# Order of the last inverse groups and four patch-row buffers in a two-layer convolution and spectral-gating kernel

## The chip, the cores and the metric

The kernel runs on one core of one Trainium2 chip. The metric is the device time of one execution in microseconds (us), the median of several runs. The kernel is one program for the five engines of the core, each with its own in-order queue: TensorE (PE in the profile), VectorE (DVE), ScalarE (ACT), GpSimd (POOL) and SyncE (SP), which issues all DMAs. They wait for each other on semaphores alone.

## The reference, cut to what matters

The input is x of shape (16, 32, 128, 128), float32. Layer 0 is a depthwise 3x3 convolution with weights mixed per image, and a 1x1 convolution. Layer 1 is the one that the change touches:

```python
def _L1_conv_ref(x, w_hidden, w_dw, norm_w, norm_b, w_out, patch_size):
    hidden = jnp.einsum('oc,bchw->bohw', w_hidden, x)          # 32 -> 192 channels
    hidden = conv(hidden, w_dw, 3x3, depthwise, 'SAME')
    q, k, v = jnp.split(hidden, 3, axis=1)                     # 64 channels each
    q_fft = jnp.fft.rfft2(to_patch(q))                         # patches of 8 x 8 pixels
    k_fft = jnp.fft.rfft2(to_patch(k))
    out = jnp.fft.irfft2(q_fft * k_fft, s=(p, p))
    mu, var = out.mean(axis=1), out.var(axis=1)                # over channels, per pixel
    out_norm = (out - mu) / jnp.sqrt(var + 1e-05) * norm_w + norm_b
    gated = v * out_norm
    return jnp.einsum('oc,bchw->bohw', w_out, gated)

x = x + _L0_conv_ref(_gn(x), ...)
x = x + _L1_conv_ref(_gn(x), ...)
```

## The kernel before, in words

The first phase (about the first 560 us) does layer 0 for all 16 images and stores the normalised result, split in a high and a low float16 part, padded, to DRAM. The second phase does layer 1 in 32 units, u = 0 to 31, each of half an image: 8 patch rows of 16 patches. Transforms are done as matmuls, on windows of 10 x 10 pixels (a patch and its border), so that the depthwise convolution is folded into the matrices `G_q` and `G_k`.

A unit has two halves on every engine, written out by hand in the functions `front` and `spectral`:

- `front(u, half, tail)` makes the hidden channels of unit u and at the same time finishes unit u - 1, the tail. VectorE's `window` (line 1099) copies one patch row of 16 overlapping windows from `xs` into a buffer `win`; there are two, and the copy of row r first waits until the hidden groups of row r - 2 are done. TensorE's `hidden_group` (line 558), four groups for each patch row, 32 in all, multiplies it; ScalarE (line 811) moves the result into `hwin`. For the tail, VectorE takes pixel statistics of `Y` (line 1109), hands the variance to POOL for the root (lines 1115 and 441), centres (1122) and scales (1129) in eight pieces p = 0 to 7; TensorE's `turn` (line 590) transposes a piece, ScalarE (820) copies it to `gated`, VectorE's `gate` (1134) multiplies it by v, and TensorE's `project` (599) applies `w_out`; VectorE's `residual` (1141) adds it to the image. v itself comes from `v_chunk` (line 577), 18 matmuls of 512 columns for each of eight chunks, into three banks in turn. Between the taps of a chunk stand the hidden groups.
- `spectral(u, half, tail)` transforms q (line 637, eight octets) and k (line 654, sixteen quads), VectorE multiplies them (line 1199, sixteen products, two for each of four buffers `prod`), TensorE transforms back (line 670, `inverse_octet`, eight groups), and ScalarE copies the result to `Y` (line 865). Groups 0 to 5 stand in pairs between the quads. Behind the last quad TensorE does `v_chunk` 0 of this unit, with the wait for the last product and for `Y` ahead of its last tap, then groups 6 and 7. VectorE copies patch rows 0 and 1 of the next unit behind products 8 and 11.

`front` of TensorE then goes on with two hidden groups, `v_chunk` 1 with four more between its taps, `turn` of piece 0, `v_chunk` 2 with five, `turn` of piece 1, and so on; a `project` stands ahead of `turn` 2, 4 and 6, and `turn` 7 stands behind the first q octet of `spectral`. `v_chunk` 1 and 2 wait for ScalarE's last two copies to `Y`, since these share their banks; later chunks wait for the gate of the chunk two before; a `project` waits for both gates that it uses. In the order before, VectorE's front copies patch row 2 behind the scale of piece 0, row 3 behind the scale of piece 1, and rows 4 to 7 at the ends of steps p = 1 to 4, each behind that step's gate, centre, scale and, where there is one, residual.

The first unit has no tail: its copies stand beside the last statistics of the first phase. The last `front` has no hidden groups and only finishes unit 31.

Of the kernel before, what the change touches and what calls it, by code (L numbers as in the profile page):

```python
# [63 lines left out]
def build(nc, t, out):  # L64
# [22 lines left out]
    with ctx:  # L87
# [177 lines left out]
        hwin = take(128 * 128)  # L265
        Y = take(64 * 64)
        q_sb = [take(512) for _ in range(2)]
        prod = [take(1024) for _ in range(4)]
        gated = [take(512) for _ in range(2)]
        res = take(2048)  # L270
        xs_1, xs_0 = [take(HALF * WP, f16) for _ in range(2)]
# [1 line left out]
        assert stage1_end <= top[0] - (HALF * WP + 1) // 2  # L273
        G_q = take(64 * 64)
        G_k = take(64 * 128)
        win = [take(1632, f16) for _ in range(2)]

        block = ctx.enter_context(nc.Block())
# [126 lines left out]
        @block.gpsimd  # L406
        def _(pool):

            pool.memset(powers, -0.5).then_inc(s_pool_consts, 1)
            pool.memset(ones_row, 1.0).then_inc(s_pool_consts, 1)  # L410
            for s in range(3):
                pool.memset(xq[s][0:32, 0:W], 0.0).then_inc(s_x_edges, 1)
                pool.wait_ge(s_x_edges, 2 * s + 1)
                pool.memset(xq[s][96:128, (BAND - 1) * W:BAND * W], 0.0).then_inc(s_x_edges, 1)
                pool.wait_ge(s_x_edges, 2 * s + 2)
            pool.wait_ge(s_prep_v, 1)
            pool.memset(xh.bitcast(f32), 0.0).then_inc(s_pads_zero, 1)
            pool.memset(xl.bitcast(f32), 0.0).then_inc(s_pads_zero, 1)
            for s in range(2):
                pool.memset(win[s][:, 16 * WIN:1632].bitcast(f32), 0.0).then_inc(s_win_room, 1)  # L420
            pool.wait_ge(s_pool_consts, 2)
            pool.wait_ge(s_pads_zero, 2)
            pool.wait_ge(s_win_room, 2)

            for b in range(-1, NB + 1):
                pool.wait_ge(s_ve, b + 2)
                pool.tensor_tensor(tiny["rstds"], tiny["ve"], powers[:, 0:2], ALU.pow).then_inc(s_rstd, 1)
                pool.wait_ge(s_rstd, b + 2)
                if b + 1 < NB:
                    pool.wait_ge(s_centred, 4 * (b + 1) + 1)  # L430
                    pool.memset(xq[(b + 1) % 3][0:32, 0:W], 0.0).then_inc(s_halo_zero, 1)
                    pool.wait_ge(s_halo_zero, 2 * (b + 1) + 1)
                    pool.wait_ge(s_centred, 4 * (b + 1) + 4)
                    pool.memset(xq[(b + 1) % 3][96:128, (BAND - 1) * W:BAND * W], 0.0).then_inc(s_halo_zero, 1)
                    pool.wait_ge(s_halo_zero, 2 * (b + 2))
# [13 lines left out]
        def _(pe):  # L449
# [94 lines left out]
            def hidden_group(u, g, ring):  # L544
# [6 lines left out]
                    pe.wait_ge(s_x2_ready, NCH * NB)  # L551
                if positive(32 * u + g + 1 - ring):
                    pe.wait_ge(s_h_ready, 32 * u + g + 1 - ring)
                w = win[g // 4 % 2]
                for i in range(4):
                    first = (4 * (g % 4) + i) * WIN
                    for low, high in ((0, 64), (64, WIN)):
# [4 lines left out]
            def v_chunk(u, half, k, jr, groups, between, before_last=None):  # L562

                chunk = 2 * k + jr
                if chunk == 0:
# [3 lines left out]
                if chunk > 2:  # L569
                    pe.wait_ge(s_gated, 8 * u + chunk - 2)  # L570
                for tap in range(9):
                    if tap == 8 and before_last is not None:
                        before_last()
                    dy, dx = tap // 3, tap % 3
                    for s in range(2):
                        row = 8 * (2 * s + jr) + dy
# [52 lines left out]
            def spectral(u, half, tail):  # L629
# [36 lines left out]
                def inverse_octet(m):  # L666
                    for part in range(2):
                        for par in range(2):
                            for lam in range(2):
                                mm = pe.matmul(i_banks[par][64 * lam:64 * lam + 64, 256 * (m % 2):256 * (m % 2) + 256],  # L670
                                               small["inverse"][64 * par:64 * par + 64, 64 * part:64 * part + 64],
                                               at(prod[m % 4][64 * par:64 * par + 64, :], 256 * part + 64 * lam, [512, 2], [128, 2], [1, 64]),
                                               start=part == 0, stop=part == 1)
                    mm.then_inc(s_inverse_mm, 1)

# [4 lines left out]
                for m in range(8):  # L680
# [8 lines left out]
                    k_quad(2 * m + 1)  # L689
                    if m == 0 and tail is not None:  # L690
                        project(tail, 3)
                v_chunk(u, half, 0, 0, 0, None, lambda: inverse_inputs(7))
                inverse_octet(6)
                inverse_octet(7)

            front(0, 0, None)
            spectral(0, 0, None)
# [184 lines left out]
        def _(dve):  # L882
# [209 lines left out]

            def window(u, half, r, b=None):

                if positive(32 * u + 4 * (r - 1)):
                    dve.wait_ge(s_hidden_mm, 32 * u + 4 * (r - 1))
                if r == 0:
                    dve.wait_ge(s_xs_in[half], 64 * (b + 1))
                dve.tensor_copy(win[r % 2][:, 0:16 * WIN].rearrange("p (j y x) -> p j y x", y=10, x=10),  # L1099
                                     at(xs[half], 8 * r * WP, [8, 16], [WP, 10], [1, 10])).then_inc(s_win_ready, 1)  # L1100

            def pixel_stats(u, p):
# [38 lines left out]
                dve.tensor_tensor(piece, banks[6].rearrange("p (l r w) -> p l r w", l=2, r=8), piece, ALU.add).then_inc(s_res_done, 1)  # L1141

            def front(u, half, tail):
                rows = iter(range(2, 8) if u is not None else ())

                def windows(n=1):
                    for r in islice(rows, n):
# [2 lines left out]
                if tail is None:  # L1150
                    second_stats(NB - 1, range(4, NCH))
                    aggregate(NB + 2, NB - 1, None)
                    windows(2)
                    quarter_variance(NB + 2, None)
                    low(NB - 2, 0)
                    low(NB - 2, 1)
# [11 lines left out]
                    if p == 1:  # L1168
                        centre(tail, 0)
                scale(tail, 0)  # L1170
                windows()
                centre(tail, 1)
                scale(tail, 1)
                windows()
                for p in range(8):
                    if p < 5:
                        pixel_stats(tail, p + 3)
                        variance(tail, p + 3)
                    if p < 7 or u is None:
                        gate(tail, p // 2, p % 2)  # L1180
                    if p < 6:
# [1 line left out]
                        scale(tail, p + 2)  # L1183
                    if p in (2, 4, 6):
                        residual(tail, p // 2 - 1)
                    if p > 0:
                        windows()

            def spectral(u, tail, nxt):
                if tail is not None:  # L1190
                    gate(tail, 3, 1)
                for n in range(16):
                    m, second = n // 2, n % 2
                    dve.wait_ge(s_q_copied, 8 * u + m + 1)
                    dve.wait_ge(s_k_mm, 16 * u + n + 1)
                    if positive(8 * u + m - 3):
                        dve.wait_ge(s_inverse_mm, 8 * u + m - 3)
                    parts = lambda a: a.rearrange("p (part x) -> p part x", part=2)
                    dve.tensor_tensor(parts(prod[m % 4][:, 512 * second:512 * second + 512]), parts(k_banks[n % 3]),  # L1199
                                      q_sb[m % 2][:, 256 * second:256 * second + 256].unsqueeze(1).broadcast_to([128, 2, 256]),  # L1200
                                      ALU.mult).then_inc(s_prod_ready, 1)
                    if n == 1 and tail is not None:
                        residual(tail, 3)
                    if nxt is not None and n in (8, 11):
                        window(nxt[0], nxt[1], (n - 8) // 3, nxt[2])

            dve.wait_ge(s_win_room, 2)
            window(0, 0, 0, 0)
            window(0, 0, 1, 0)
# [54 lines left out]
```

## Time and profile before

| | |
|---|---|
| median of three runs | 2808.57 us |
| lowest and highest | 2798.39 and 2824.54 us |
| the profiled execution's own time | 2816.34 us |
| its span, first to last instruction | 2814.5 us |
| TensorE matmuls busy | 2513.6 us, 89% |
| VectorE, ScalarE, GpSimd busy | 59%, 51%, 17% |
| mean granted TensorE clock | 0.965 of full speed |

Shares are of the span. Matmuls are pipelined and their ends are modelled, so the busy share of TensorE is no measure of how near to its peak it is. "Idle before" an instruction is the time in which its engine had nothing running ahead of it; the releaser named is what ended that time.

### The profile page before, as it was taken

The numbers are of one execution on the slowest core, as the hardware profiler recorded it, in microseconds if no ns is written. First come the engines' busy times: TensorE is split into PE (matmuls) and PEld (weight loads), VectorE is DVE, ScalarE is ACT, GpSimd is POOL, SyncE is SP. The second block draws the span as 40 slices with busy tenths as digits, with TensorE's granted clock in tenths as the row PEclk, the third lists the DMA queues.
The fourth block names the chain that finished last, engine by engine and source line by source line (L and its number), as shares of the span: only waits on it lengthen the run. The fifth ranks groups of instructions, "written<-read, shape, count | busy, mean of one in ns | idle before, by whom it ended". The sixth has DMA issues, their size and how long they took to land.

```text
span 2814.5 us, 90655 instructions
## 1 busy us (share of the span) xinstructions
PE 2513.6 (89%) x40199; PEld 1659.2 (59%) x40199; DVE 1650.5 (59%) x4058; ACT 1440.8 (51%) x2381; POOL 471.8 (17%) x322
## 2 busy tenths in 40 slices
PE   7888889789999999999999899998999989999998
PEld 3333333466666666666666666666666666666665
DVE  4656666455555555555555556555555555656555
ACT  3545555645455555555555455555555555555552
POOL 1000000021111212112121112122212122212221
PEclk9988988899999999999999999999999999999999
DMA  6788887622222222222222222222222222222221
GB/s 128 184 214 202 213 227 203 165 66 62 57 63 59 63 63 67 63 59 67 59 67 63 59 63 63 63 65 61 67 63 66 61 62 66 68 60 67 63 52 46
DMA packets 60345, 248.30 MB, mean 88 GB/s; under 512 B 12393, under 2 KB 12658, under 8 KB 53714
## 3 DMA queue, kind: packets, MB, share of 16 engines
q1 hardware_dynamic: 59954, 242.50, 35.3%
q8 instruction: 317, 5.19, 0.8%
q14 instruction: 74, 0.61, 0.1%
HBM read 140.74 MB, written 101.72 MB: 86 GB/s over the span
## 4 chain that ended last, share of the span: by engine, by line
PE 58%; DVE 14%; ACT 5%; issue 3%; SPq 0%; DMA 0%; DVEq 0%
PE bank L654 16%; PE bank L577 11%; PE bank L670 9%; PE bank L637 7%; PE bank L590 6%; PE bank L558 5%; ACT arena L820 4%; PE bank L599 4%; DVE arena L1109 3%; DVE arena L1122 3%; DVE arena L1134 2%; DVE arena L1129 2%; DVE arena L1099 2%; DVE arena L1141 2%; ACT arena L865 1%
## 5 line engine op out<-in xcount | busy, mean ns | idle before, releaser
L441 POOL TENSOR_TENSOR arena<-arena 128x8 f32<-128x8 f32 x256 | 447.6, 1748 | 1814.8 <-DVE arena L1115 1809.8
L577 PE MATMUL bank<-arena 128*64 128x512 f16 x4608 | 713.4, 403 | 5.5 <-ACT arena L865 5.5
L811 ACT ACTIVATE arena<-bank 100x512 f32<-100x512 f32 x1024 | 615.7, 630 | 183.8 <-PE bank L558 166.7
L1199 DVE TENSOR_TENSOR arena<-bank,arena 128x512 f32<-128x512 f32 x512 | 354.1, 692 | 457.4 <-PE bank L654 370.6
L558 PEld LDWEIGHTS bank<-arena 128*36 128x36 f16 (+1 forms) x8192 | 332.0, 106 | 382.5 <-DVE arena L1099 157.8
L654 PE MATMUL bank<-arena 100*64 100x128 f32 x8192 | 513.1, 274 | 15.4 <-issue 8.7
L558 PE MATMUL bank<-arena 128*36 128x128 f16 (+1 forms) x8192 | 406.1, 224 | 122.1 <-DVE arena L1099 115.8
L654 PEld LDWEIGHTS bank<-arena 100*64 100x64 f32 x8192 | 457.5, 136 | 54.4 <-issue 47.3
L512 PE MATMUL bank<-arena 32*32 32x508 f32 (+1 forms) x9216 | 389.7, 660 | 57.7 <-issue 42.9
L820 ACT ACTIVATE arena<-bank,arena 128x256 f32<-128x256 f32 x512 | 261.1, 560 | 191.6 <-PE bank L590 189.6
L865 ACT ACTIVATE arena<-bank 128x512 f32<-128x512 f32 x256 | 139.1, 596 | 406.1 <-PE bank L670 406.1
L1134 DVE TENSOR_TENSOR arena<-arena,bank 128x512 f32<-128x512 f32 x256 | 176.0, 687 | 270.1 <-ACT arena L820 268.7
L857 ACT ACTIVATE arena<-bank 128x512 f32<-128x512 f32 x256 | 149.2, 598 | 338.6 <-PE bank L637 325.2
L1109 DVE BATCH_NORM_STATS2 arena<-arena 128x6 f32<-128x128 f32 x1024 | 221.9, 279 | 139.2 <-ACT arena L865 139.2
L637 PE MATMUL bank<-arena 100*64 100x128 f32 x4096 | 274.3, 275 | 4.7 <-ACT arena L857 3.2
L512 PEld LDWEIGHTS bank<-arena 32*32 32x32 f32 x9216 | 142.7, 108 | 207.2 <-issue 177.2
L577 PEld LDWEIGHTS bank<-arena 128*64 128x64 f16 x4608 | 211.2, 112 | 87.8 <-ACT arena L865 11.0
L670 PE MATMUL bank<-arena 64*64 64x256 f32 x4096 | 254.8, 383 | 1.3 <-issue 1.3
L637 PEld LDWEIGHTS bank<-arena 100*64 100x64 f32 x4096 | 233.2, 137 | 30.6 <-issue 17.9
L590 PE MATMUL bank<-arena 128*128 128x128 f32 x1024 | 181.9, 301 | 66.6 <-DVE arena L1129 59.9
L590 PEld LDWEIGHTS bank<-arena 128*128 128x128 f32 x1024 | 133.8, 195 | 167.2 <-DVE arena L1129 101.2
L670 PEld LDWEIGHTS bank<-arena 64*64 64x64 f32 x4096 | 143.6, 131 | 84.4 <-issue 32.7
(112 smaller groups left out, 1620.6 us busy)
## 6 DMA issues: line engine op xcount, KB each, us to landing
arena<-xn_d SPq DMA_DIRECT2D x128, 536.2 KB, 8.3
xn_d<-arena SPq DMA_DIRECT2D x130, 260.0 KB, 4.5
x_d<-arena SPq DMA_DIRECT2D x64, 512.0 KB, 8.3
arena<-x_d SPq DMA_DIRECT2D x128, 256.0 KB, 4.9
out<-arena SPq DMA_DIRECT2D x128, 256.0 KB, 5.3
arena<-x_in SPq DMA_DIRECT2D x32, 544.0 KB, 10.1
arena<-x_in SPq DMA_DIRECT2D x32, 528.0 KB, 10.0
arena<-spectra_in SPq DMA_DIRECT2D x1, 1152.0 KB
```

What stands on the lines that cost most here:

```text
L441: pool.tensor_tensor(tiny["rstd"][:, slot], tiny["var_eps"][:, slot], powers, ALU.pow).then_inc(s_root, 1)
L512: mm = pe.matmul(at(psum_of(t, r)[32 * c:32 * c + 32, :], low, [W, 4], [1, high - low]), conv_w[b % 2][32 * r:32 * r + 32, 32 * tap:32 * t ...
L558: mm = pe.matmul(banks[g % ring][low:high, 128 * i:128 * i + 128], w[:, first + low:first + high], hidden_w, start=True, stop=True)
L577: mm = pe.matmul(v_banks[chunk % 3][64 * s:64 * s + 64, :], v_w[:, 64 * tap:64 * tap + 64], at(xs[half], row * WP + 32 * k + dx, [32 * WP, ...
L590: tr = pe.transpose(t_bank[:, 128 * i:128 * i + 128], at(Y, 8 * k + 4 * jr + i, [32, 128]), ident)
L637: mm = pe.matmul(banks[m % 2][64 * par:64 * par + 64, 128 * pair:128 * pair + 128], G_q[0:WIN, 64 * ch:64 * ch + 64], hwin[0:WIN, 128 * ch ...
L654: mm = pe.matmul(k_banks[n % 3][64 * par:64 * par + 64, 256 * part + 128 * pair:256 * part + 128 * pair + 128], G_k[0:WIN, 128 * ch + 64 * ...
L670: mm = pe.matmul(i_banks[par][64 * lam:64 * lam + 64, 256 * (m % 2):256 * (m % 2) + 256], small["inverse"][64 * par:64 * par + 64, 64 * pa ...
L811: act.activation(h_rows[0:WIN, :, first:first + 4], banks[g % ring][0:WIN, :].rearrange("p (i c) -> p c i", i=4), ACT.Copy).then_inc(s_h_r ...
L820: ins = act.activation(at(gated[jr], 256 * lam, [32, 8], [8, 4], [1, 8]), at(banks[4], 64 * lam, [8, 8], [128, 4], [1, 8]), ACT.Identity, ...
L1109: ins = dve.bn_stats(T["pixel_stats"][:, first:first + 6], at(Y, 2048 * s + 4 * p + j, [32, 64], [1, 2]))
L1199: dve.tensor_tensor(parts(prod[m % 4][:, 512 * second:512 * second + 512]), parts(k_banks[n % 3]), q_sb[m % 2][:, 256 * second:256 * secon ...
```

## The change

TensorE: behind the last k quad the last two inverse groups come at once, each behind its own wait, and `v_chunk` 0 follows them. VectorE: four `win` buffers instead of two, so the copy of row r waits for the hidden groups of row r - 4. Rows 0 to 3 of the next unit are copied behind products 8, 10, 11 and 13, row 4 behind the scale of piece 1, and rows 5 to 7 in steps p = 1 to 3, now ahead of that step's gate. Products go round three buffers instead of four, and wait for one inverse group more. For the first unit rows 0 to 3 are copied ahead of `front`.

```diff
-        prod = [take(1024) for _ in range(4)]
+        prod = [take(1024) for _ in range(3)]
...
-        win = [take(1632, f16) for _ in range(2)]
+        win = [take(1632, f16) for _ in range(4)]
...
@@ hidden_group
-                w = win[g // 4 % 2]
+                w = win[g // 4 % 4]
@@ v_chunk
-                    if tap == 8 and before_last is not None:
-                        before_last()
@@ inverse_octet
-                                               at(prod[m % 4][64 * par:64 * par + 64, :], ...),
+                                               at(prod[m % 3][64 * par:64 * par + 64, :], ...),
@@ spectral, TensorE
-                v_chunk(u, half, 0, 0, 0, None, lambda: inverse_inputs(7))
+                pe.wait_ge(s_prod_ready, 16 * u + 14)
+                pe.wait_ge(s_y_ready, 8 * u + 6)
                 inverse_octet(6)
+                pe.wait_ge(s_prod_ready, 16 * u + 16)
                 inverse_octet(7)
+                v_chunk(u, half, 0, 0, 0, None)
@@ window
-                if positive(32 * u + 4 * (r - 1)):
-                    dve.wait_ge(s_hidden_mm, 32 * u + 4 * (r - 1))
+                if positive(32 * u + 4 * (r - 3)):
+                    dve.wait_ge(s_hidden_mm, 32 * u + 4 * (r - 3))
@@ front, VectorE
-                rows = iter(range(2, 8) if u is not None else ())
+                rows = iter(range(4, 8) if u is not None else ())
...
                     aggregate(NB + 2, NB - 1, None)
-                    windows(2)
                     quarter_variance(NB + 2, None)
...
                 scale(tail, 0)
-                windows()
                 centre(tail, 1)
                 scale(tail, 1)
                 windows()
                 for p in range(8):
                     if p < 5:
                         pixel_stats(tail, p + 3)
                         variance(tail, p + 3)
+                    if p > 0:
+                        windows()
                     if p < 7 or u is None:
                         gate(tail, p // 2, p % 2)
...
                         residual(tail, p // 2 - 1)
-                    if p > 0:
-                        windows()
@@ spectral, VectorE
-                    if positive(8 * u + m - 3):
-                        dve.wait_ge(s_inverse_mm, 8 * u + m - 3)
+                    if positive(8 * u + m - 2):
+                        dve.wait_ge(s_inverse_mm, 8 * u + m - 2)
...
-                    if nxt is not None and n in (8, 11):
-                        window(nxt[0], nxt[1], (n - 8) // 3, nxt[2])
+                    if nxt is not None and n in (8, 10, 11, 13):
+                        window(nxt[0], nxt[1], (8, 10, 11, 13).index(n), nxt[2])
```

## Rows read from the trace of the kernel before

**Rows 1.** The page: granted clock in 40 slices; shares of the chain that ended last.
```profile
PEclk9988988899999999999999999999999999999999
...
PE 58%; DVE 14%; ACT 5%; issue 3%; SPq 0%; DMA 0%; DVEq 0%
```

**Rows 2.** Waits of TensorE, 700 to 2600 us: total, times, longest.
```profile
PE bank L558 <- DVE arena L1099: 97.2, 81, 1.6
PE bank L590 <- DVE arena L1129: 49.8, 27, 1.9
...
PE bank L577 <- ACT arena L865: 4.2, 27, 0.2
```

**Rows 3.** Timeline of TensorE in one unit: start, length, what, [idle before, releaser].
```profile
1437.28 2.23 PE L577 MATMUL bank<-arena 128*64 128x512 f16 x18
1439.44 1.98 PE L670 MATMUL bank<-arena 64*64 64x256 f32 x32
1441.34 0.64 PE L558 MATMUL bank<-arena 128*64 128x128 f16 x16
1442.13 0.88 PE L577 MATMUL bank<-arena 128*64 128x512 f16 x6 [0.15 <-ACT arena L865]
...
1447.12 0.71 PE L590 MATMUL bank<-arena 128*128 128x128 f32 x4 [1.85 <-DVE arena L1129]
...
1454.90 1.02 PE L599 MATMUL bank<-arena 128*64 128x512 f32 x4
...
1459.25 0.39 PE L577 MATMUL bank<-arena 128*64 128x512 f16 x2
1460.89 0.41 PE L558 MATMUL bank<-arena 128*64 128x128 f16 x8 [1.25 <-DVE arena L1099]
...
1465.66 0.41 PE L558 MATMUL bank<-arena 128*64 128x128 f16 x8 [0.88 <-DVE arena L1099]
...
1471.90 0.41 PE L558 MATMUL bank<-arena 128*64 128x128 f16 x8 [1.47 <-DVE arena L1099]
...
1478.51 0.68 PE L590 MATMUL bank<-arena 128*128 128x128 f32 x4 [0.18 <-ACT arena L820]
```

**Rows 4.** Timeline of VectorE in the same unit.
```profile
1435.81 0.69 DVE L1199 TENSOR_TENSOR arena<-bank,arena 128x512 f32<-128x512 f32 x1 [2.24 <-PE bank L654]
...
1437.55 0.69 DVE L1199 TENSOR_TENSOR arena<-bank,arena 128x512 f32<-128x512 f32 x1 [0.18 <-PE bank L654]
1442.60 0.88 DVE L1109 BATCH_NORM_STATS2 arena<-arena 128x6 f32<-128x128 f32 x4 [4.36 <-ACT arena L865]
...
1446.38 0.69 DVE L1129 TENSOR_TENSOR arena<-arena 128x512 f32<-128x512 f32 x1
1446.98 0.57 DVE L1099 COPY arena<-arena 128x1600 f16<-128x1600 f16 x1
...
1452.91 0.87 DVE L1109 BATCH_NORM_STATS2 arena<-arena 128x6 f32<-128x128 f32 x4
...
1460.27 0.57 DVE L1099 COPY arena<-arena 128x1600 f16<-128x1600 f16 x1
```

**Rows 5.** Timeline of ScalarE in the same unit.
```profile
1434.74 1.09 ACT L865 ACTIVATE arena<-bank 128x512 f32<-128x512 f32 x2 [2.20 <-PE bank L670]
```

**Rows 6.** Timeline of GpSimd in the same unit.
```profile
1445.55 4.44 POOL L441 TENSOR_TENSOR arena<-arena 128x8 f32<-128x8 f32 x2
...
1451.07 1.64 POOL L441 TENSOR_TENSOR arena<-arena 128x8 f32<-128x8 f32 x1 [1.09 <-DVE arena L1115]
```

**Rows 7.** Stretches: all 31 units, one undisturbed unit, two at the lower clock.
```profile
core 0: us, PE busy (x) PEld busy (x) DVE busy (x) ACT busy (x) POOL busy (x), PEclk, DMA share, GB/s
595.35:2773.48 2178.13, 1989.09 (x29760) 1419.54 (x29756) 1283.14 (x3098) 1114.76 (x1984) 434.25 (x248) 0.99 0.26 62
1441.48:1510.51 69.03, 63.26 (x966) 45.30 (x964) 41.44 (x100) 35.80 (x65) 14.17 (x8) 1.00 0.27 64
670.89:674.30 3.41, 3.41 (x36) 2.13 (x34) 1.86 (x6) 2.12 (x4) 1.65 (x1) 0.50 0.02 5
2500.44:2503.85 3.41, 3.41 (x29) 1.92 (x30) 1.68 (x4) 2.21 (x4) 1.90 (x1) 0.50 0.00 0
```

More of the change, by code:

```diff
@@ L418, in _ @@
             pool.memset(xl.bitcast(f32), 0.0).then_inc(s_pads_zero, 1)
-            for s in range(2):
+            for s in range(4):
                 pool.memset(win[s][:, 16 * WIN:1632].bitcast(f32), 0.0).then_inc(s_win_room, 1)
@@ L422, in _ @@
             pool.wait_ge(s_pads_zero, 2)
-            pool.wait_ge(s_win_room, 2)
+            pool.wait_ge(s_win_room, 4)
             for b in range(-1, NB + 1):
@@ L560, in hidden_group, with v_chunk @@
                 mm.then_inc(s_hidden_mm, 1)
-            def v_chunk(u, half, k, jr, groups, between, before_last=None):
+            def v_chunk(u, half, k, jr, groups, between):
                 chunk = 2 * k + jr
@@ L671, in inverse_octet @@
                                                small["inverse"][64 * par:64 * par + 64, 64 * part:64 * part + 64],
-                                               at(prod[m % 4][64 * par:64 * par + 64, :], 256 * part + 64 * lam, [512, 2], [128, 2], [1, 64]),
+                                               at(prod[m % 3][64 * par:64 * par + 64, :], 256 * part + 64 * lam, [512, 2], [128, 2], [1, 64]),
                                                start=part == 0, stop=part == 1)
@@ L1093, in window @@
             def window(u, half, r, b=None):
-                if positive(32 * u + 4 * (r - 1)):
-                    dve.wait_ge(s_hidden_mm, 32 * u + 4 * (r - 1))
+                if positive(32 * u + 4 * (r - 3)):
+                    dve.wait_ge(s_hidden_mm, 32 * u + 4 * (r - 3))
                 if r == 0:
                     dve.wait_ge(s_xs_in[half], 64 * (b + 1))
-                dve.tensor_copy(win[r % 2][:, 0:16 * WIN].rearrange("p (j y x) -> p j y x", y=10, x=10),
+                dve.tensor_copy(win[r % 4][:, 0:16 * WIN].rearrange("p (j y x) -> p j y x", y=10, x=10),
                                      at(xs[half], 8 * r * WP, [8, 16], [WP, 10], [1, 10])).then_inc(s_win_ready, 1)
@@ L1195, in spectral @@
                     dve.wait_ge(s_k_mm, 16 * u + n + 1)
-                    if positive(8 * u + m - 3):
-                        dve.wait_ge(s_inverse_mm, 8 * u + m - 3)
+                    if positive(8 * u + m - 2):
+                        dve.wait_ge(s_inverse_mm, 8 * u + m - 2)
                     parts = lambda a: a.rearrange("p (part x) -> p part x", part=2)
-                    dve.tensor_tensor(parts(prod[m % 4][:, 512 * second:512 * second + 512]), parts(k_banks[n % 3]),
+                    dve.tensor_tensor(parts(prod[m % 3][:, 512 * second:512 * second + 512]), parts(k_banks[n % 3]),
                                       q_sb[m % 2][:, 256 * second:256 * second + 256].unsqueeze(1).broadcast_to([128, 2, 256]),
@@ L1203, in spectral @@
                         residual(tail, 3)
-                    if nxt is not None and n in (8, 11):
-                        window(nxt[0], nxt[1], (n - 8) // 3, nxt[2])
-            dve.wait_ge(s_win_room, 2)
-            window(0, 0, 0, 0)
-            window(0, 0, 1, 0)
+                    if nxt is not None and n in (8, 10, 11, 13):
+                        window(nxt[0], nxt[1], (8, 10, 11, 13).index(n), nxt[2])
+            dve.wait_ge(s_win_room, 4)
+            for r in range(4):
+                window(0, 0, r, 0)
             front(0, 0, None)
```

## The prediction

> **What bounds the kernel now.** I first read the busy line of the clock and the chain that ended last [rows 1]: the clock is at its upper level outside the first fifth, and over half of the chain is TensorE, with VectorE second. The kernel spends 2178.13 us of its 2814.5 us in 31 equal units of the second phase [rows 7]; the stretch before them (595 us) and after them (41 us) is hardly touched by the diff. A unit without disturbance takes 69.03 us [rows 7]. So the question is what TensorE does in one unit.
>
> The list of waits over 1900 us, 27 units, answers: TensorE waits for the patch-row copies of line 1099 97.2 us (81 times, three in a unit), for `y_norm` of line 1129 49.8 us (27 times) and for ScalarE's Y copies 4.2 us [rows 2]. The timeline of one unit shows the places [rows 3]. Let T0 be the end of the last inverse group, 1441.34. There are 0.15 us of wait before the next `v_chunk`, 1.85 us before the first `turn`, 1.25, 0.88 and 1.47 us before the hidden groups that open patch rows 5, 6 and 7, and 0.18 us before the last `turn`. The spectral half in front of T0 runs without a gap worth naming.
>
> How long is a wait really? Two matmuls start at 1459.25 and the next group at 1460.89 [rows 3]. Two of them cost 0.23 us when others follow directly, so the wait costs 1.41 us and not the recorded 1.25. In the same way 0.88 becomes 1.04, 1.47 becomes 1.63, 1.85 becomes 2.01, and 0.15 becomes 0.34. The Trainium skill says so too (Perfetto Trace Analysis, Identifying the Most-Contended Engine): matmul busy time is a poor measure because matmuls are pipelined. By recorded idle alone the five waits would be worth 5.6 us a unit, by starts 6.4; the trace agrees with the page, and my sum is made from starts.
>
> **Part 1: inverse groups first, then `v_chunk(0)`.** Now `v_chunk(0)` takes 1437.28 to 1439.44, 2.16 us, and the two inverse groups 1.90 us behind it [rows 3]. After T0 a chain starts that no order on TensorE shortens: ScalarE's two copies, VectorE from 1442.60 (statistics, centre, scale), scale at 1446.38 for 0.69 us [rows 4], and `turn` at 1447.12, T0 + 5.78 [rows 3]. TensorE has only 3.4 us of other work for it. With `v_chunk(0)` behind T0 it has 2.16 + 0.45 (two hidden groups) + 2.98 (`v_chunk(1)` with four) = 5.59 us. The chain is still last by about 0.2 us, so `turn` stays at T0 + 5.78, and the whole 2.16 us, now spent in the chain's shadow, is gained.
> What it adds is a wait. Group 6 needs product 14, done at 1435.81 + 0.69 = 1436.50 [rows 4], and Y copies that end at 1435.83 [rows 5], so it starts at 1437.28 and ends near 1438.23. Group 7 needs the last product, 1437.55 + 0.69 = 1438.24 [rows 4]. Everything on TensorE queues behind this wait. A release is followed by TensorE 0.05 us later (1447.07 to 1447.12), and a wait costs some 0.15 us more than it records, as above. So it costs between 0.06 and 0.4 us (a pipeline drain plus a short stall, as the 0.34 of the Y copies); I take 0.15, as the wait is all but met when it is reached. Net gain: 2.0 us.
>
> **Part 2: four patch-row buffers, copies ahead of the gates.** The three waits cost 1.41 + 1.04 + 1.63 = 4.08 us. Does the copy come in time? In the order before, rows 2 and 3 are copied in the busiest stretch of VectorE (1446.98) and row 5 at 1460.27, T0 + 18.93, behind a residual, while TensorE asks for it at 1459.64 [rows 3, 4]. In the new order rows 0 to 3 are done in the spectral half, where VectorE idles 2.24 us before a product [rows 4]. A copy occupies 0.49 us from start to start. The statistics of step 4 start at 1452.91, T0 + 11.57 [rows 4]. Ahead of them two copies and the 0.41 us wait in front of the second fall away and one copy comes: they start at T0 + 10.7, and row 5 is copied at T0 + 11.7. Row 6 follows one step (3.5 us) later, row 7 one more (4.2 us, with a residual and a gate that waits): about T0 + 15.2 and 20.0. TensorE, dense from `turn` on, asks for them at about T0 + 18.3, 21.8 and 26.2. Margins are 6 us, so all three waits go. The waits that the copies themselves carry (4, 8, 12, 16 hidden groups done) are met 3 us or more ahead.
> What is late next? The gates. `project(0)` starts at T0 + 13.56 (1454.90) [rows 3] and needs gate 1, which I get at T0 + 12.1 + 0.7 = 12.8: 0.7 us of margin. The same walk over the orders of the two engines leaves 0.8 and 0.9 us at `project(1)` and `project(2)`, where VectorE itself again waits for ScalarE. The chunk that needs gate 0 has 1.0 us. POOL's second root ends near T0 + 5.9, 0.5 us ahead of its scale. So nothing new shows in TensorE, but nothing is wide.
>
> **Part 3: copies in the spectral half** now behind products 8, 10, 11 and 13. Behind product 13 the copy pushes product 14 from 1436.68 to 1436.91 and product 15 would then be free at 1437.52, before its own quad is done at 1437.55 [rows 4]. Behind product 10 product 11 comes 0.2 us later, while the inverse group that reads it is reached 0.3 us after that. Cost 0, with 0.1 us as the bound. Row 0 waits for the load of the next half image, which was so before at the same product.
>
> **Part 4: three product buffers.** Product m now waits for m - 2 inverse groups. Groups 0 and 1 are done before product pair 4 and groups 2 and 3 before pair 5 is needed; group 4 before pair 7. The wait is met each time by one pair at least: 0. Moved addresses and two more small memsets on POOL at the start: 0; the fourth removed edit, `before_last`, belongs to part 1. In the first unit four copies stand in an idle stretch of VectorE instead of two: 0.
>
> **Sum.** A unit gives 2.0 + 4.08 = 6.1 us; 31 units 189 us; the clock 24 us; T0 of the first unit 2 us earlier; the last front 0 (its chain also ends at T0 + 5.78 + what follows). 215 us from the profiled execution's own 2816.34 us gives 2601 us. That execution lies 8 us above the median of the runs, 2808.57; as the clock's falls differ by chance and mostly go, I take off only a little: 2600 us.
>
> **Rivals.**
> (A) The falls of the clock stay, or a gate margin turns into a short wait. The clock may fall after shorter pauses once they stand alone; against it, no fall follows the three waits of up to 1.47 us. 2601 + 24 = 2625 us; with another 0.3 us in each unit 2634.
> (B) The copies get in each other's way with POOL. The new copies of rows 5 to 7 stand directly behind the statistics that release POOL's root. The rows show that a copy and a root do touch: the two roots that ran beside the copies of patch rows 2 and 3 took 2.22 us each, one with no copy beside it 1.64 [rows 6], but the copy itself was not held (1446.98, 0.57 us, started within a running root) [rows 4]. If copies were held for a whole root, each would come 1.6 us late, the gate behind it too, past the 0.7 us margin: about 1 us for each of three steps, 3 us a unit, 93 us: near 2695 us. The Trainium skill states this rule (SBUF, Who interferes with whom): whichever of a two-port VectorE copy and a GpSimd instruction issues first blocks the other fully. The trace disagrees for the copy here and shows only a partial delay for POOL.
> (C) Part of it only: the copies help, but the wait is moved from `turn` to inverse group 7 or gate 0, so that part 1 gives nothing: 31 x 2.0 = 62 us less and the falls stay: 2687 us. Against it is the count above, 1438.23 against 1438.24.
> (D) Slower: a denser TensorE is not granted the upper clock. Place: the front half, now without pauses. A fall of 3.41 us costs 1.6 us, so it decides between four and five falls in each unit: four (13.6 us of 63 at the lower level) leave 2799 us, five give 2601 + 31 x 5 x 1.6 = 2849 us. Against it: the spectral half is gapless now, and no fall starts in it.
>
> **Chances.** Forecast 0.66, A 0.20, B 0.04, C 0.06, D 0.03, the remaining 0.01 for no change. The range takes the forecast with its bounds (the new wait at 0.4 us adds 8 us; the clock of the first phase and the median 15 us either way) and A: 2582 to 2638 us. Faster by over 1% 0.96, within 1% 0.01, slower 0.03; 1% is about what the spread of the three runs before lets one tell from nothing.
>
> **What would show it.** In the profile after: no TensorE wait for line 1099's copies in the units; the wait at the first `turn` under 0.4 us with `turn` still 5.8 us behind the last inverse group; a new short wait of the inverse groups for the last product; units of 63 us; the clock at its upper level after 600 us. Wrong would be the gate margins, if waits appear at `project`; the clock, if falls go on; and VectorE's walk, if copies are late.

## The result, and the profile after

The changed kernel takes 2595.18 us (median of 4 runs, 2584.55 to 2598.81), the kernel before 2807.22 us (4 runs). The ratio is 0.9231 with a 95% interval of 0.9179 to 0.9284. The profiled execution took 2592.72 us with a span of 2590.9 us, 223.6 us less than that of before.

The page after, busy line of TensorE, granted clock in 40 slices, and shares of the chain that ended last:

```profile
PE 2463.1 (95%) x40199; PEld 1648.5 (64%) x40199; DVE 1638.2 (63%) x4058; ACT 1447.8 (56%) x2381; POOL 476.4 (18%) x324
...
PEclk9989898879999999999999999999999999999999
...
PE 69%; DVE 6%; ACT 2%; issue 1%; SPq 0%; DMA 0%; ACTq 0%
```

Against [rows 1] TensorE's share of the chain has gone from 58% to 69% and VectorE's from 14% to 6%: the chain now stays on TensorE. The waits of TensorE from 700 to 2400 us (total, times, longest):

```profile
PE bank L652 <- issue: 6.5, 5, 1.6
PE bank L588 <- ACT arena L821: 4.8, 27, 0.2
```

Both large entries of [rows 2] are gone. What is left is 0.18 us in each unit at the last `turn` (line 588 now, 590 before) and a few waits for instructions ("issue"). All 31 units, and one undisturbed unit, in the view of stretches:

```profile
core 0: us, PE busy (x) PEld busy (x) DVE busy (x) ACT busy (x) POOL busy (x), PEclk, DMA share, GB/s
591.26:2551.64 1960.38, 1943.09 (x29762) 1408.84 (x29760) 1270.16 (x3096) 1121.86 (x1984) 438.80 (x248) 1.00 0.29 69
1348.82:1411.66 62.84, 62.54 (x962) 45.32 (x961) 41.00 (x100) 36.18 (x65) 14.15 (x8) 1.00 0.30 71
```

A unit takes 62.84 us instead of 69.03, and all 31 take 1960.38 instead of 2178.13 us [rows 7]. One unit in TensorE's timeline (start, length, what):

```profile
1343.96 2.84 PE L652 MATMUL bank<-arena 100*64 100x128 f32 x48
1346.73 2.02 PE L668 MATMUL bank<-arena 64*64 64x256 f32 x32
1348.68 2.25 PE L575 MATMUL bank<-arena 128*64 128x512 f16 x18
1350.77 0.61 PE L558 MATMUL bank<-arena 128*64 128x128 f16 x16
...
1353.95 0.39 PE L558 MATMUL bank<-arena 128*64 128x128 f16 x8
1354.46 0.71 PE L588 MATMUL bank<-arena 128*128 128x128 f32 x4
...
1362.23 1.03 PE L597 MATMUL bank<-arena 128*64 128x512 f32 x4
1363.19 0.71 PE L588 MATMUL bank<-arena 128*128 128x128 f32 x4
...
1366.81 0.39 PE L558 MATMUL bank<-arena 128*64 128x128 f16 x8
...
1370.52 0.39 PE L558 MATMUL bank<-arena 128*64 128x128 f16 x8
...
1375.10 0.39 PE L558 MATMUL bank<-arena 128*64 128x128 f16 x8
```

The last inverse groups come at 1346.73, `v_chunk` 0 and 1's first taps behind them at 1348.68, which is the new T0. The first `turn` starts at 1354.46, T0 + 5.78, exactly as in [rows 3], but the list of waits has none there any more. The hidden group of 1353.95 starts 0.51 us ahead of it, and a group ahead of a `turn` that waits for nothing starts some 0.32 us ahead (1366.81 to 1367.13 further on), so about 0.2 us are left of the wait. The hidden groups that open patch rows 5, 6 and 7 stand at 1366.81, 1370.52 and 1375.10, each the last of its chunk, and wait for nothing. VectorE in the same unit:

```profile
1345.16 0.69 DVE L1198 TENSOR_TENSOR arena<-bank,arena 128x512 f32<-128x512 f32 x1 [2.24 <-PE bank L652]
1345.76 0.57 DVE L1100 COPY arena<-arena 128x1600 f16<-128x1600 f16 x1
1346.25 1.35 DVE L1198 TENSOR_TENSOR arena<-bank,arena 128x512 f32<-128x512 f32 x2
1349.94 0.87 DVE L1110 BATCH_NORM_STATS2 arena<-arena 128x6 f32<-128x128 f32 x4 [2.34 <-ACT arena L866]
...
1353.71 0.69 DVE L1130 TENSOR_TENSOR arena<-arena 128x512 f32<-128x512 f32 x1
...
1355.72 0.57 DVE L1100 COPY arena<-arena 128x1600 f16<-128x1600 f16 x1
...
1360.31 0.57 DVE L1100 COPY arena<-arena 128x1600 f16<-128x1600 f16 x1
1360.80 0.68 DVE L1135 TENSOR_TENSOR arena<-arena,bank 128x512 f32<-128x512 f32 x1
...
1363.85 0.57 DVE L1100 COPY arena<-arena 128x1600 f16<-128x1600 f16 x1
...
1368.65 0.57 DVE L1100 COPY arena<-arena 128x1600 f16<-128x1600 f16 x1
```

Row 3 of the next unit is copied at 1345.76 between products, and the last two products run back to back from 1346.25; rows 4 to 7 are copied at T0 + 7.0, 11.6, 15.2 and 20.0. Gate 1 at 1360.80 ends 0.75 us ahead of `project(0)` at 1362.23. Line 1100 is the copy, 1110 the statistics, 1130 the scale, 1135 the gate.

Where the 223.6 us come from, by the two traces: the 31 units 217.75 us, of which 31 x 6.19 = 191.9 us are the shorter undisturbed unit and the other 25.9 us are the disturbances above it, 38.2 us before and 12.3 us after; the stretch ahead of the units 4.1 us, and the one behind them 1.8 us. The last of these goes with the clock: behind its last unit the kernel before has three stretches at the lower level (from 2780.3, 2804.2 and 2811.0 us), the changed kernel one (from 2586.7). The kernel before with three product buffers, a run below, has only one too and takes 39.3 us behind its units, as the changed kernel does, and not 41.0.

### The profile page after: what moved, and what is told of

Its sections match the earlier page's. It is cut to its first block, busy times and chain, and to the rows that moved or that the text cites. A ratio compares the mean times of both kernels' runs of the same rounds, so it can differ in the third digit from the quotient of the medians.

```text
span 2590.9 us, 90657 instructions
## 1 busy us (share of the span) xinstructions
PE 2463.1 (95%) x40199; PEld 1648.5 (64%) x40199; DVE 1638.2 (63%) x4058; ACT 1447.8 (56%) x2381; POOL 476.4 (18%) x324
## 4 chain that ended last, share of the span: by engine, by line
PE 69%; DVE 6%; ACT 2%; issue 1%; SPq 0%; DMA 0%; ACTq 0%
PE bank L652 18%; PE bank L575 16%; PE bank L668 10%; PE bank L635 8%; PE bank L558 7%; PE bank L588 7%; PE bank L597 4%; DVE arena L1110 3%; ACT arena L866 1%; DVE arena L1130 1%; ACT arena L821 1%; DVE arena L1123 1%; DVE arena L1116 0%; DVE arena L1118 0%; SPq L318 0%
## 5 line engine op out<-in xcount | busy, mean ns | idle before, releaser
L575 PE MATMUL bank<-arena 128*64 128x512 f16 x4608 | 694.4, 393 | 0.0
L558 PEld LDWEIGHTS bank<-arena 128*64 128x64 f16 (+1 forms) x8192 | 333.7, 104 | 231.5 <-issue 4.3
L558 PE MATMUL bank<-arena 128*64 128x128 f16 (+1 forms) x8192 | 394.1, 220 | 10.2 <-DVE arena L1100 4.2
L575 PEld LDWEIGHTS bank<-arena 128*64 128x64 f16 x4608 | 204.3, 109 | 88.7 <-issue 12.4
L1130 DVE TENSOR_TENSOR arena<-arena 128x512 f32<-128x512 f32 x256 | 177.4, 693 | 23.4
```

The lines of the kernel that those rows point to most:

```text
L558: mm = pe.matmul(banks[g % ring][low:high, 128 * i:128 * i + 128], w[:, first + low:first + high], hidden_w, start=True, stop=True)
L575: mm = pe.matmul(v_banks[chunk % 3][64 * s:64 * s + 64, :], v_w[:, 64 * tap:64 * tap + 64], at(xs[half], row * WP + 32 * k + dx, [32 * WP, ...
```

## The experiments

The median of a whole run moves by some 10 us without a cause in the units: T0 of the first unit lies between 578.5 and 597.9 us in the thirteen traces of this study, which is the first phase, not touched here. So each experiment is read first by its shortest unit, which repeats to 0.02 us, and then by its median. "Unit" below is that shortest unit of the profiled execution. A "fall" is a stretch in the 31 units in which the granted clock is at its lower level, and falls too are counted in the one profiled execution. Each ratio is to 9 to 13 runs of the kernel before, made beside that experiment (medians 2806 to 2811 us).

### The new order alone

The kernel before with this edit and nothing else:

```diff
-                v_chunk(u, half, 0, 0, 0, None, lambda: inverse_inputs(7))
+                pe.wait_ge(s_prod_ready, 16 * u + 14)
+                pe.wait_ge(s_y_ready, 8 * u + 6)
                 inverse_octet(6)
+                pe.wait_ge(s_prod_ready, 16 * u + 16)
                 inverse_octet(7)
+                v_chunk(u, half, 0, 0, 0, None)
```

> The kernel before with the new order of TensorE alone: inverse groups 6 and 7 directly behind the last quad, v_chunk 0 behind them; two patch-row buffers, copies where they were. My account: the chain from the last inverse group to the first turn is fixed (5.78 us), so 2.1 us of each unit go, from 69.03 to 66.9 us; the waits of 1.25, 0.88 and 1.47 us for the copies stay as they are, since VectorE's list is fixed to the same chain. The wait ahead of the first turn falls to about 0.2 us, and the clock no longer falls in the units: some 24 us more. 2807 - 65 - 24 - 2 = 2716 us. Rival 1: the falls of the clock have nothing to do with the wait at turn; then they stay and the time is 2740 us. Rival 2: TensorE's earlier work only makes it wait longer at the copies; then unit 69.0 and 2780 to 2807 us.

Measured: 2724.22 us, ratio 0.9698 (0.9672 to 0.9724), unit 66.99 us, and no fall of the clock in the 31 units. TensorE's waits from 700 to 2400 us, 25 units:

```profile
PE bank L558 <- DVE arena L1102: 90.1, 75, 1.6
PE bank L654 <- issue: 7.6, 5, 1.9
PE bank L590 <- ACT arena L823: 4.4, 25, 0.2
```

The wait of 1.85 us at `turn` is gone and the three waits for copies stand as they were, 3.6 us a unit. So the order gives 2.03 us of a unit (2.1 expected), and the falls go with it. The median lies 8 us above the expectation and 16 us under rival 1, which it alone would hardly rule out; the trace does, as no unit has a fall. Rival 2 is out by the unit.

### The copies alone

The changed kernel with the old order at the end of TensorE's spectral half (the edit above, backwards).

> The changed kernel with the old order of TensorE at the end of the spectral half (v_chunk 0 ahead of the last two inverse groups); four patch-row buffers, early copies and three product buffers stay. My account: the three waits for copies go, 4.1 us of each unit, from 69.03 to 64.95 us; the wait of 1.85 us at the first turn stays and so do the falls of the clock, in about half of the units at 1.6 us. 2807 - 126 = 2681 us. Rival: the clock fell because of all the waits of a unit together; then the falls go with the copies' waits and the time is 2657 us, with the 1.85 us still there.

Measured: 2669.58 us, ratio 0.9512 (0.9489 to 0.9534), unit 64.87 us.

```profile
PE bank L590 <- DVE arena L1129: 48.1, 26, 1.9
...
PE bank L577 <- ACT arena L865: 4.0, 26, 0.2
```

No wait for a copy is left, and the waits at `turn` and for the Y copies are those of before. The copies give 4.15 us of a unit; 2.03 + 4.15 = 6.18 against 6.19 for both, so the parts add up. The median is 11 us under the expectation, which had counted on falls in about half of the units: only 6 came behind `turn`, and a seventh elsewhere. Nine falls fewer than 15 are 9 x 1.6 = 14 us of the profiled execution, which took 2675.77 us where 2816.34 - 126 = 2690 would have kept all of them. The wait had its old length; why fewer falls follow it, this run does not tell.

### Copies behind the gates

The changed kernel, copies of rows 5 to 7 at the end of their step:

```diff
-                    if p > 0:
-                        windows()
                     if p < 7 or u is None:
                         gate(tail, p // 2, p % 2)
...
                         residual(tail, p // 2 - 1)
+                    if p > 0:
+                        windows()
```

> The changed kernel with the copies of rows 5 to 7 again at the end of their step, behind gate, centre, scale and residual; everything else as changed. My account: the copies then land about 3 us later, at T0 + 15, 19 and 23, against 18.3, 21.8 and 26.2 when they are asked for, so no wait comes back: unit 62.8 us, 2595 us. Rival: it is the place ahead of the gates that cures the waits; then the waits come back in part, 1 to 4 us in a unit, 2625 to 2720 us.

Measured: 2596.3 us, ratio 0.9241 (0.9216 to 0.9266), unit 62.84 us: the same as the changed kernel. VectorE's copies of rows 4 to 7, in a unit with T0 at 1337.98:

```profile
1345.02 0.57 DVE L1100 COPY arena<-arena 128x1600 f16<-128x1600 f16 x1
...
1351.62 0.57 DVE L1100 COPY arena<-arena 128x1600 f16<-128x1600 f16 x1
...
1356.91 0.57 DVE L1100 COPY arena<-arena 128x1600 f16<-128x1600 f16 x1
...
1360.45 0.57 DVE L1100 COPY arena<-arena 128x1600 f16<-128x1600 f16 x1
```

They start at T0 + 7.0, 13.6, 18.9 and 22.5, and TensorE asks for rows 5 to 7 at T0 + 18.1, 21.8 and 26.4 (the rows of the changed kernel at 1366.81, 1370.52 and 1375.10 above). Even 2.9 us from the start of a copy to the demand for it are enough. The place ahead of the gates gains nothing here. This unit has no fall; one came elsewhere (see the last section).

### Four buffers with the copies at their old places

The kernel before with four patch-row and three product buffers; rows 0 and 1 in the spectral half, 2 to 7 in front, as before.

```diff
-        prod = [take(1024) for _ in range(4)]
+        prod = [take(1024) for _ in range(3)]
...
-        win = [take(1632, f16) for _ in range(2)]
+        win = [take(1632, f16) for _ in range(4)]
...
-                if positive(32 * u + 4 * (r - 1)):
-                    dve.wait_ge(s_hidden_mm, 32 * u + 4 * (r - 1))
+                if positive(32 * u + 4 * (r - 3)):
+                    dve.wait_ge(s_hidden_mm, 32 * u + 4 * (r - 3))
...
```

> The kernel before with four patch-row buffers and three product buffers, but each copy at its old place in VectorE's list (rows 0 and 1 in the spectral half, 2 to 7 in front). My account: only VectorE's own wait of 0.41 us ahead of row 3 goes, so all later copies come 0.4 us earlier and the first of TensorE's three waits shrinks by that, the later ones perhaps not: 0.4 to 0.8 us of a unit, 2807 - 12 to 25 = 2782 to 2795 us. Rival: the number of buffers is what cures the waits; then unit 64.9 us and 2670 us.

Measured: 2804.39 us, ratio 0.9979 (0.9957 to 1.0001), unit 69.02 us, 12 falls: no gain clear of the noise, less than I had expected. VectorE, in an undisturbed unit with T0 at 1286.55 (copy of row 3, gates 1 and 2, residual, copy of row 5), and TensorE's first wait for a copy in it:

```profile
1294.08 0.57 DVE L1099 COPY arena<-arena 128x1600 f16<-128x1600 f16 x1
...
1298.68 0.68 DVE L1134 TENSOR_TENSOR arena<-arena,bank 128x512 f32<-128x512 f32 x1
...
1302.89 0.69 DVE L1134 TENSOR_TENSOR arena<-arena,bank 128x512 f32<-128x512 f32 x1 [0.58 <-ACT arena L820]
...
1304.89 0.68 DVE L1141 TENSOR_TENSOR arena<-bank,arena 128x512 f32<-128x512 f32 x1
1305.49 0.57 DVE L1099 COPY arena<-arena 128x1600 f16<-128x1600 f16 x1
```
```profile
1306.11 0.41 PE L558 MATMUL bank<-arena 128*64 128x128 f16 x8 [1.25 <-DVE arena L1099]
```

Row 3 no longer waits: its copy starts at T0 + 7.53 instead of 8.02, and gate 1 follows early too. But gate 2 then waits 0.58 us for ScalarE's copy of a turned piece and starts at T0 + 16.34, as before (1457.66 in the unit of [rows 4] is T0 + 16.32), and the copy of row 5, which stands behind it, starts at T0 + 18.94 against 18.93. So it hangs on TensorE's own `turn`, by way of ScalarE and the gate, and TensorE's wait keeps its 1.25 us. Time saved ahead of a waiting gate is lost in its wait. The buffers are still needed for the new places: with two, the copy of row 2 waits for the hidden groups of row 0, which stand in `front`, so rows 2 and 3 could not be copied in the spectral half. No run has the new places without the buffers.

### Three product buffers alone

> The kernel before with three product buffers and nothing else. My account: each product's wait for the inverse groups is met long before, so nothing changes: unit 69.03 us, 2807 us. Rival: products wait for inverse groups and the next quads for them; then a VectorE wait at the products for line 670 shows in the profile and a unit is up to 2 us longer, 2870 us.

Measured: 2806.29 us, ratio 1.0007 (0.9986 to 1.0028), unit 69.01 us, 15 falls of the clock, 14 of them behind the first `turn`. The smaller ring costs nothing. It is what makes the room: by the sizes in the code, four product and four patch-row buffers would need an arena of 53806 words, and it is 53200 long.

### Gate 1 later by 1.5 us

The changed kernel with eight more statistics, written to spare words, ahead of those of step 4; p == 0 takes the place of p == 4 in the four runs on the first `turn`.

```diff
             def pixel_stats(u, p):
...
+                if p == 4 and u < LAST:
+                    for i in range(8):
+                        dve.bn_stats(spare[:, 6 * i:6 * i + 6], at(Y, 2048 * (i // 2 % 2) + 4 * p + 2 * (i % 2), [32, 64], [1, 2]))
```

> The changed kernel with eight more statistics ahead of those of step 4, so gate 1 comes 1.8 us later; the output does not use them. It measures the margin of 0.7 us at project 0. My account: TensorE waits at project 0 for 1.8 - 0.75 = 1.05 us, some 1.2 by starts; the later gates keep their margins, as they wait for ScalarE. Unit 64.0 us, 2595 + 37 = 2632 us. Rival: VectorE has room to take it; then nothing, 2595 us. Second rival: the margins fall one after the other and each later step gets late by 1 us; then 2660 to 2690 us.

Measured: 2617.25 us, ratio 0.9316 (0.9275 to 0.9357), unit 63.73 us. Eight statistics turned out to delay gate 1 by 1.54 us and not 1.8 (T0 + 13.66 instead of 12.12). TensorE, `project(0)` and the `turn` behind it, then the weight loads of the same `project`:

```profile
1428.01 1.91 PE L598 MATMUL bank<-arena 128*64 128x512 f32 x4
1429.85 0.71 PE L589 MATMUL bank<-arena 128*128 128x128 f32 x4
```
```profile
1427.96 0.20 PEld L598 LDWEIGHTS bank<-arena 128*64 128x64 f32 x2
1428.85 0.19 PEld L598 LDWEIGHTS bank<-arena 128*64 128x64 f32 x2 [0.69 <-DVE arena L1139]
```

`project` has two halves, each with its own gate, which otherwise run side by side in 0.96 us (1362.23 to 1363.19 in the changed kernel). Here the second half's weights wait until 1428.85, when gate 1 is done, and the whole takes 1.84 us. 1.54 us of delay cost 0.89 us of the unit, so the margin was 0.65 us; 0.7 was forecast. Nothing more was lost later in the unit: the second rival is out, and so is the first. The expectation, with 1.8 us of delay, was 64.0 us for the unit and 2632 us.

### The first turn later, by four lengths

Four, eight, ten and fourteen more statistics of piece 0, to lengthen the wait at the first `turn` in the changed kernel and see when the clock falls.

> As the run with 1.8 us, with four more statistics: the first turn 0.9 us later, its wait 1.1 us by starts. My account: a unit of 63.7 us and no fall, since no fall followed the waits of 0.88 to 1.47 us in the kernel before: 2595 + 28 = 2623 us. Rival: any wait at this place lets the clock fall; then 2630 to 2645 us.

> The changed kernel with eight more statistics of piece 0 on VectorE, into spare words, ahead of the real ones (units 1 to 31; the output does not use them). Eight times 0.225 us: the first turn comes 1.8 us later, so its wait is as long as in the kernel before (1.85 us), in an otherwise changed kernel. My account: a unit of 62.84 + 1.8 = 64.6 us, and the falls of the clock behind this wait come back, in 7 (as with the copies alone) to 15 units: 2595 + 56 + 11 to 24 = 2662 to 2675 us. Rival: the falls belong to the sum of a unit's waits; then none, 2651 us.

> The changed kernel with ten more statistics ahead of the first turn. Eight of them moved the turn by 1.54 us (0.193 us each), made a wait of 1.66 us and no fall of the clock; ten make a wait of 2.05 us, longer than the 1.85 us of the kernel before. My account, that it is the length of this one wait that matters: falls come back, at least the 6 of 31 units seen with the copies alone; unit 64.77 us, 2595 + 60 + 10 to 24 = 2665 to 2679 us. Rival, that the waits in the rest of the unit or the short one ahead of v_chunk 1 are needed too: no fall, 2655 us.

> The same with fourteen more statistics: wait of 2.8 us, as long as in the last front of the kernel before, which has a fall behind it. My account: falls in at least as many units as with ten, up to all 31; unit 65.5 us, 2595 + 84 + 10 to 50 = 2689 to 2729 us. Rival: no fall, 2679 us.

The waits for line 1134 (the scale of piece 0) from 700 to 2400 us with eight, ten and fourteen, total, times, longest:

```profile
PE bank L589 <- DVE arena L1134: 43.2, 26, 1.7
```
```profile
PE bank L589 <- DVE arena L1134: 53.4, 26, 2.1
```
```profile
PE bank L589 <- DVE arena L1134: 70.6, 25, 2.8
```

| more statistics | wait at turn, us | unit, us | falls in 31 units | median, us | ratio to before |
|---|---|---|---|---|---|
| 0 (changed kernel) | none listed | 62.84 | 0 | 2595.18 | 0.9231 |
| 4 | 0.9 | 63.61 | 0 | 2629.61 | 0.935 (0.9301 to 0.94) |
| 8 | 1.66 | 64.38 | 0 | 2639.42 | 0.9389 (0.9339 to 0.9438) |
| 10 | 2.05 | 64.77 | 11 | 2669.97 | 0.9516 (0.949 to 0.9542) |
| 14 | 2.8 | 65.54 | 19 | 2709.97 | 0.967 (0.9641 to 0.97) |

The expectation for eight was wrong: no fall came behind waits of 1.66 us (its median, 2639.42 us, lies 12 us under its rival's 2651), and that alone left open whether the other waits of a unit were needed. Ten and fourteen settle it. Falls come back in a kernel that has no other regular wait of size, and more of them behind the longer wait. But it is a matter of how often: with ten, all 31 units have the same wait and 11 have a fall, and the runs do not show what picks them. Each costs 1.6 us (66.38 against 64.78 us in the trace with ten). With four the median, 2629.61 us, lies 10 us above 2595 + 31 x 0.77 us; its units in the profiled execution are nearly as forecast (63.61 us, 63.7 expected) and that execution took 2613.33 us, so the difference is not in the units that were recorded.

### The last turn later

The changed kernel with turn 7 behind the second q octet and the last `project` behind the third:

```diff
                 q_octet(0)
-                if tail is not None:
-                    turn(tail, 3, 1)
                 for m in range(8):
                     if m < 7:
                         q_octet(m + 1)
+                    if m == 0 and tail is not None:
+                        turn(tail, 3, 1)
+                    if m == 1 and tail is not None:
+                        project(tail, 3)
...
-                    if m == 0 and tail is not None:
-                        project(tail, 3)
```

> The changed kernel with turn 7 behind the second q octet instead of the first and the last project behind the third octet. The 0.18 us of wait for ScalarE at turn 7 (0.3 us by starts) is the last regular wait of TensorE besides the first turn. My account: it goes, and gate 7, project and residual, 0.9 us later, still stand ahead of what needs them: unit 62.5 us, 2595 - 9 = 2586 us. Rival: the quads wait for the later gate or copy instead; then unit 62.8 to 63.3 us, 2595 to 2610 us.

Measured: 2578.17 us (2574.98 to 2582.76, 5 runs), ratio 0.9193 (0.9174 to 0.9213), unit 62.62 us. What is left of TensorE's waits from 700 to 2400 us:

```profile
PE bank L652 <- issue: 2.6, 4, 0.9
PE bank L668 <- issue: 1.8, 3, 1.2
```

The regular wait for ScalarE at the last `turn` is gone. The unit gains 0.22 us, where 0.3 was expected. That is 7 us of 31 units; the median fell by 17 us, 8 us under the expected 2586, and the rest of it is not in the units. All five runs lie under all four of the changed kernel, though the intervals of the two ratios overlap. This is the fastest version of the study.

## Why the prediction was right, point by point

- The bound. TensorE's waits, measured from start to start, were the right currency: five waits of 6.4 us by starts and 5.6 us as recorded, of which all but 0.2 us went, while about 0.15 us came (next point). That makes 6.1, and the unit gained 6.19 us. The recorded idle could not have given that.
- Part 1 was forecast at 2.0 us and gave 2.03 (the order alone). The chain from T0 to the first `turn` kept its 5.78 us to the hundredth. What the new order adds was put at 0.15 us, all of it the wait of group 7. In sum this was right: of 2.16 us moved, 2.03 were gained, so it costs 0.13. But most of it stands at another place. The two groups now take 1.95 us (1346.73 to 1348.68) and took 1.90, so the wait of group 7 costs 0.05 us. The other 0.10 comes one step earlier, where group 6 follows the k quads: their 48 matmuls take 2.77 us from start to the next start (1343.96 to 1346.73), and took 2.67 when `v_chunk` 0 followed (1434.61 to 1437.28, in the row below). That the total fits is in part luck.

```profile
1434.61 2.84 PE L654 MATMUL bank<-arena 100*64 100x128 f32 x48
```

- Part 2 was forecast at 4.08 us and gave 4.15 (the copies alone). The copies were forecast at T0 + 11.7, 15.2 and 20.0 and stand at 11.63, 15.17 and 19.97. The reason given was right in its main point, that rows 2 and 3 leave the front and each later row moves up by a step. It gave too much to the place ahead of the gates, which is worth nothing here, and did not say that row 5's lateness hung on TensorE through gate 2. That is why the expectation for four buffers and old places missed: 0.4 to 0.8 us of a unit expected, 0.0 measured.
- Parts 3 and 4 cost nothing, as said. With the copy behind product 13 the last two products start at 1346.25 and, back to back, some 0.65 us later, and the ring of three alone left the unit at 69.01 us.
- The clock. 15 falls, 24 us forecast; all 15 went, and the disturbances above the undisturbed units fell by 25.9 us, with 12.3 us left (14 forecast). That the falls hang on the wait at the first `turn` is shown by the order alone (no falls), the copies alone (falls stay) and the runs with a later turn. That none at all was left had some luck in it: three other runs have one fall each behind a wait for instructions, as the last section tells, and such waits stay in the changed kernel too.
- The margins of the gates. 0.7 us at `project(0)` forecast, 0.75 read, 0.65 measured by using it up.
- The rivals. (A) did not come. (B) is refuted by the trace: the 256 copies last 565 to 577 ns (561 to 579 before), although those of rows 5 to 7 stand next to a root, and that of row 4 (1355.72) starts inside the third root of the first row here. The next two rows show a root with no copy beside it and one with a copy:

```profile
1351.16 5.34 POOL L441 TENSOR_TENSOR arena<-arena 128x8 f32<-128x8 f32 x3 [40.28 <-DVE arena L1116]
1357.42 1.64 POOL L441 TENSOR_TENSOR arena<-arena 128x8 f32<-128x8 f32 x1 [0.92 <-DVE arena L1116]
1360.47 1.90 POOL L441 TENSOR_TENSOR arena<-arena 128x8 f32<-128x8 f32 x1 [1.42 <-DVE arena L1116]
```

  So it is the root that is delayed, by 0.26 us, and no one waits for it: all 124 roots that share time with a copy take 1.90 us or a little more, and all but one of the other 132 take 1.64. With the copies of rows 5 to 7 behind the gates, those roots are back at 1.64 us and the unit is the same. The prediction's 2.22 us for each of two roots before was half of a row of two; singly they take 2.05 and 2.31 us. The Trainium skill (SBUF — State Buffer, Who interferes with whom) states a full block for whichever of a two-port VectorE copy and a GpSimd instruction issues second; of this, the runs show a partial delay for GpSimd and none for the copy. (C) is refuted by the order alone, (D) by the granted clock, 1.00 over all 31 units in a denser TensorE.
- The sum. 215 us off the profiled execution were forecast, 223.6 measured. Of the 8.6 us between them, the shorter unit gives 2.9 (191.9 instead of 189), the disturbances 1.9 (25.9 instead of 24), and the stretches before and behind the units 3.9 (5.9 instead of 2). The 4.1 us before the units are within what the first phase moves from run to run, so the 2 us forecast there are neither shown nor refuted; the 1.8 us behind them go with falls of the clock, as the run with three product buffers shows, and the forecast had 0 there.

## What to carry to other kernels

Read the waits of the bounding engine by starts, and for each ask which engine's queue it hangs on; then move independent work of the bounding engine behind the instruction that starts the long chain, and move feeder copies to a stretch where their engine idles. A copy that stands behind a waiting instruction in its queue isn't helped by more buffers alone; it needs another place, and that place may need the buffers. And count what a pause costs beyond its length: here a pause of 1.85 us was followed, in some of the units, by a fall of the clock that cost another 1.6 us.

## What the runs showed of the hardware

```profile
2394.13 0.73 PE L652 MATMUL bank<-arena 100*64 100x128 f32 x6 [1.68 <-issue]
```

- Two matmul groups of `project`, 64 output rows each, run side by side in 0.96 us, and one after the other in 1.84 us with a wait between them. The wait hardly shows in the matmul rows (0.4 us in all from 700 to 2400 us), but it does in the weight loads (0.69 us in the unit shown).
